# Attention results kept as channel rows through HBM, and a head's value product in two bursts

## What is computed

```python
def proj(W, b):
    return (x @ W.T + b).reshape(B, S, H, hd).transpose(0, 2, 1, 3)
Q, K, V = (proj(Wq, bq), proj(Wk, bk), proj(Wv, bv))
scores = jnp.einsum('bhqd,bhkd->bhqk', Q, K) * scale
attn = jax.nn.softmax(scores, axis=-1)
out = jnp.einsum('bhqk,bhkd->bhqd', attn, V)
out = out.transpose(0, 2, 1, 3).reshape(B, S, D)
return out @ Wo.T + bo
```

## Time and profile before

| | |
|---|---|
| time, three runs | 2012.56, 2013.42, 2052.93 us (median 2013.42) |
| profiled execution, its own time | 2010.89 us |
| its span, first to last instruction | 2008.9 us |
| granted TensorE clock over the span | 0.940 |
| busy: PE, DVE, ACT, POOL | 88%, 57%, 44%, 20% |
| head loop, first unit to last value product | 103.7 to 896.5 us |
| output projection, to the last statistics | 897 to 942 us |
| experts, wavelet, experts | 942 to 2008.9 us |

### The profile page before, as it was taken

How to read it: one execution, slowest core, us unless ns; L and a number is a source line. 1 busy time by engine, 2 the same in 40 slices (tenths; PEclk the granted TensorE clock), 3 DMA queues, 4 the chain that set the end, 5 groups by cost and what they waited for, 6 DMA issues and landing times. The chain is left out here.

```text
span 2008.9 us, 36274 instructions
## 1 busy us (share of the span) xinstructions
PE 1763.1 (88%) x11202; PEld 1122.9 (56%) x11203; DVE 1146.1 (57%) x2473; ACT 887.8 (44%) x1306; POOL 408.6 (20%) x573
## 2 busy tenths in 40 slices
PE   7999999999999999988479999999999579944772
PEld 4523444444444444437368888888888546943551
DVE  4688888888888888846821111111111287797223
ACT  3436666666666666664112333333332144230223
POOL 2310000000000000003013333333333100000782
PEclk9969999999999999999789999999999879977896
DMA  5501111111111111106624443344344300024544
GB/s 196 181 18 36 36 32 32 32 32 34 35 34 32 32 32 33 35 23 201 228 86 117 101 116 104 109 110 110 111 105 114 93 6 1 2 84 147 87 54 168
DMA packets 101160, 157.44 MB, mean 78 GB/s; under 512 B 19984, under 2 KB 76624, under 8 KB 95728
## 3 DMA queue, kind: packets, MB, share of 16 engines
q1 hardware_dynamic: 70720, 120.30, 18.4%
q0 software_dynamic: 21696, 23.85, 7.5%
q10 hardware_dynamic: 8688, 12.58, 1.7%
HBM read 122.23 MB, written 48.37 MB: 85 GB/s over the span
## 5 line engine op out<-in xcount | busy, mean ns | idle before, releaser
L552 DVE TENSOR_REDUCE unit_max<-ps_ring 128x1 f32<-128x512 f32 x1024 | 639.3, 683 | 70.1 <-PE ps_ring L427 64.1
L538 ACT ACTIVATE w<-ps_scores 128x1024 f32<-128x1024 f32 x512 | 503.6, 1022 | 263.3 <-PE ps_scores L504 260.4
L427 PE MATMUL ps_ring<-k_stack,q_stack 96*128 96x512 bf16 x1024 | 367.6, 393 | 17.6 <-POOL v_padded L390 7.6
L504 PE MATMUL ps_scores<-q_stack,k_stack 98*128 98x512 bf16 x1024 | 307.5, 382 | 2.6 <-ACT w L538 2.5
L1486 PE MATMUL m_ps_h<-m_xt,m_w 128*128 128x256 f32 x1248 | 278.6, 382 | 0.8 <-DVE m_xt L1537 0.8
L1498 PE MATMUL m_ps_y<-w,m_ht 128*128 x1248 | 275.8, 379 | 0.0
L449 PE MATMUL ps_o<-w,v_padded 128*32 128x256 f32 x4096 | 261.9, 385 | 0.0
L1486 PEld LDWEIGHTS m_ps_h<-m_xt,m_w 128*128 128x128 f32 x1248 | 239.0, 192 | 34.2 <-DVE m_xt L1537 1.2
L1498 PEld LDWEIGHTS m_ps_y<-w,m_ht 128*128 128x128 f32 x1248 | 234.2, 190 | 30.3
L427 PEld LDWEIGHTS ps_ring<-k_stack,q_stack 96*128 96x128 bf16 x1024 | 98.8, 97 | 259.0 <-DVE unit_max L552 177.2
L1518 ACT ACTIVATE m_ht<-m_ps_h,m_w 128x256 f32<-128x256 f32 x312 | 130.7, 470 | 144.8 <-PE m_ps_h L1486 144.8
(11 more groups left out here) (263 smaller groups left out, 1624.2 us busy)
## 6 DMA issues: line engine op xcount, KB each, us to landing
m_w<-in_w SPq DMA_DIRECT2D x39, 1028.0 KB
rows<-g_rows SPq DMA_DIRECT2D x16, 512.0 KB, 3.0
y<-sums SPq DMA_DIRECT2D x16, 512.0 KB, 7.1
q_parts<-qk_part SPq DMA_DIRECT2D x16, 384.0 KB
k_parts<-qk_part SPq DMA_DIRECT2D x16, 384.0 KB
q_stack<-q_parts SPq DMA_DIRECT2D x64, 96.0 KB
k_stack<-k_parts SPq DMA_DIRECT2D x64, 96.0 KB
xt<-in_xt ACTq DMA_DIRECT2D x8, 512.0 KB, 10.0
```

What stands on the lines that cost most here:

```text
L427: nc.tensor.matmul(out[:, :], qs[0:STACK, u, qt * P:(qt + 1) * P], ks[0:STACK, u, half * HALF:(half + 1) * HALF], start=True, stop=True).t ...
L504: mm = nc.tensor.matmul(p_s[kt % 2][:, half * HALF:(half + 1) * HALF], ks[:, u, kt * P:(kt + 1) * P], qs[:, u, half * HALF:(half + 1) * HALF],
L538: nc.scalar.activation(pt[:, kt, :], p_s[kt % 2][:, :], ACT.Exp, scale=SCALE)\
L552: nc.vector.tensor_reduce(unit_max[:, u % 2, half, qt:qt + 1], src[:, :], axis=AX.X, op=ALU.max).then_inc(ring_used, 1)
```

## The change

1. `EDGES` becomes (0, 4, 8): the value product of a head is two bursts of four tiles, one after step 5 and one after step 1 of the next head.
2. The fold is gone, on TensorE and on VectorE. SP stores each head's copied strips to HBM as they are (`store_o`; `o_raw` holds 32 rows of 1024 queries a head, of which rows 0 to 15 are the result's channels and row 16 the divisor).
3. Groups are of `HEADS` = 8 heads; one written out, six turns of the loop, one written out. In a group SP reads back the eight heads of the group before as 128 channel rows, and their divisors as 128x64 (`load_block`). VectorE takes the reciprocal of the divisors (after head 2 of the group), SP stores it and reads it back repeated for 16 rows (`store_reciprocals`, `load_reciprocals`), and VectorE multiplies 128x1024 into `c.o_t` (`scale_block`, after head 5). The eighth block is left for the output stage.
4. At a group's last unit two places of the ring's count are skipped, so that a turn of the loop is a multiple of three: product and reduction count 3 there (`taken`).
5. `stage_output` uses `c.o_t` directly as the stationary operand: no gathering, no transposes, no copies. Wo, the bias and the first x are loaded, and their bias added, during the last group. There are four buffers of x and four PSUM banks for products, and the loops are written out.

```diff
@@ constants @@
+HEADS = 8
+BLOCKS = 8
@@ new helpers @@
+def load_block(sp, c, g):
+    raw = c.o_raw[bass.ds(g * HEADS, HEADS), :, :]
+    sp.dma_start(c.raw[:, :, :].rearrange("p j f -> p (j f)"), raw[:, 0:HD, :]).then_inc(c.raw_loaded, 16)
+    sp.dma_start(c.den[:, :], raw[:, HD, :]).then_inc(c.den_loaded, 16)
...
+def scale_block(v, c, kb):
+    def split(x):
+        return x.rearrange("p j (b q) -> p j b q", b=2)
+    return v.tensor_tensor(c.o_t[:, bass.ds(kb, 1), :].rearrange("p a (b j q) -> p (a j) b q", b=2, j=4),
+                           split(c.raw[:, :, :]), split(c.inv[:, :, :]), ALU.mult).then_inc(c.scaled, 1)
@@ stage_attention @@
-        GROUPS = NH // SLOTS
-        FOLD_AT, ROWS_AT, COPY_AT = 4, 2, 1
-        EDGES = (0, 3, 6, KT)
+        GROUPS = NH // HEADS
+        ROWS_AT, COPY_AT = 2, 1
+        SPARES = -HEADS * (2 * KT + 1) % RING
+        EDGES = (0, KT // 2, KT)
...
+        def taken(last, u, kt, kind):
+            return 1 + SPARES if (u, kt, kind, last) == (HEADS - 1, KT - 1, "max1", False) else 1
@@ SP @@
+                def store_o(n, u):
+                    sp.wait_ge(o_copied, n + 1)
+                    sp.dma_start(c.o_raw[bass.ds(n + HEADS, 1), :, :].rearrange("a r (j f) -> (a j) r f", j=4), o_sb[:, u % 2, :])\
+                        .then_inc(c.o_stored[u % 2], 16)
...
+                        if not first:
+                            if u == 1:
+                                for p in range(2):
+                                    sp.wait_ge(c.o_stored[p], g * (HEADS // 2 * 16))
+                                sp.wait_ge(c.scaled, g)
+                                load_block(sp, c, g)
+                            if u == 3:
+                                sp.wait_ge(c.inverted, g)
+                                store_reciprocals(sp, c, g)
+                            if u == 4:
+                                sp.wait_ge(c.inv_stored, g * 16)
+                                load_reciprocals(sp, c, g)
+                        if not (first and u == 0):
+                            store_o(n - 1, u + 1)
@@ TensorE @@
                             if kt == 1 and not (first and u == 0):
                                 pv(n - 1, u + 1, BURSTS - 1)
-                            if kt in (4, 7):
-                                pv(n, u, (kt - 4) // 3)
-                            emit(kt, ("fold",))
+                            if kt == 5:
+                                pv(n, u, 0)
@@ VectorE @@
-                            elif kind == "fold":
-                                normalise(n - 2, g * 2 + (u // 2 - 1), at - 1, src)
...
+                        if not first and u == 2:
+                            dve.wait_ge(c.den_loaded, g * 16)
+                            nc.vector.reciprocal(c.rden[:, :], c.den[:, :]).then_inc(c.inverted, 1)
+                        if not first and u == 5:
+                            dve.wait_ge(c.raw_loaded, g * 16)
+                            dve.wait_ge(c.inv_loaded, g * 16)
+                            scale_block(nc.vector, c, g - 1)
@@ stage_output, TensorE @@
+                for i in range(NT // 2):
+                    b, s = i // PAIRS, i % PAIRS
+                    wait_from(pe, summed, i - 3)
+                    pe.wait_ge(c.scaled, min(2 * b + 2, BLOCKS) + 1)
...
@@ stage_output, VectorE @@
+                dve.wait_ge(c.den_loaded, LAST)
+                nc.vector.reciprocal(c.rden[:, :], c.den[:, :]).then_inc(c.inverted, 1)
+                for i in range(NT // 2):
...
+                    if i == 5:
+                        dve.wait_ge(c.raw_loaded, LAST)
+                        dve.wait_ge(c.inv_loaded, LAST)
+                        scale_block(nc.vector, c, BLOCKS - 1)
```

More of the change, by code:

```diff
@@ L423, in claim, with max_unit @@
                     wait_from(pe, ring_used, at - RING + 1)
-                def max_unit(u, qt, half, at, out):
+                def max_unit(u, qt, half, at, out, count=1):
                     claim(at)
@@ L474, in body @@
                 def body(g, first, last):
-                    for u in range(SLOTS):
-                        n = g * SLOTS + u
-                        ahead = not (last and u >= 2)
+                    for u in range(HEADS):
+                        n = g * HEADS + u
+                        ahead = not (last and u >= HEADS - 2)
                         before = count_before(g, first, last, u)
@@ L702, in product @@
                                                   wo[:, k, :], start=(k == 0), stop=(k == KC - 1))
                     mm.then_inc(made, 1)
-                def pairs(b, first, last):
-                    for s in range(PAIRS):
-                        if not (last and s == PAIRS - 1):
-                            turn(b * PAIRS + s + 1, s + 1)
-                        product(b * PAIRS + s, s)
-                pe.wait_ge(loaded_w, 16)
-                turn(0, 0)
-                peeled_ends(pe, B, pairs)
```

296 lines of the change are left out of this document (135 added, 161 removed).

## The result

The changed kernel is slower: 2054.48 us median of 4 runs (2052.5 to 2055.13) against 2014.16 for the kernel before, a ratio of 1.0219, interval 1.0197 to 1.0242. The interval excludes no change; it does not quite exclude a difference under 2%. One of the four runs of before, 2052.93, was disturbed, and all ratios and intervals here are taken from undisturbed runs alone, so they are not quotients of the medians shown. The forecast was 2020 with a range from 1992 to 2038. The profiled execution has a span of 2053.1 us, 44.2 more than before.

The account below looks back on a forecast made before the run. The head loop was taken as bound by TensorE and VectorE's coupling through three banks, not either engine's work. Terms -33 + 33 + 5 + 11 + 1.5 + 0.5 - 11 = +7 on 2010.9 gave 2018, median 2020, range 1992 to 2038.

Parts of the forecast that it names:

- The coupling of the two engines by three banks: Head loop: VectorE starves during bursts, the ring holds TensorE between them; two-burst distances 1.61 or 1.56 us, heads 12.1.
- the bursts do pay: Rival, head loop: VectorE does not starve in longer bursts; 1962 us in full (chance 0.05), 1990 at half (0.11).
- 2 to 3.7 us at five jumps: Rival, loop's jumps back: TensorE and VectorE wait for the doubled body's instructions; +10 to +18 us, chance 0.20.
- The combination's distance: Head loop, VectorE: no longer behind a burst, the combination of maxima stretches a distance from 0.60 to 0.79 us.
- The two bursts: Head loop: two bursts for three make a head 12.1 us, 0.54 above one without a fold; +33 us over 61 heads.
- a turn's end: A group's last unit: TensorE's lead is lost once a group; 0.7 us times 7, +5 us (0 to 8).
- both divisions: VectorE in the loop: a block's reciprocal and multiplication stand between reductions; 1.6 us a group, +11 us for seven blocks.
- Stores and loads on SP: SP's queue ahead of the extra rows: at most 2 us of delay against some 5 of slack, 0 us.
- late rows: Rival, SP's queue: extra rows come late behind a head's store; slower than 2%, 2080 with 1 us, chance 0.04.
- The output stage: After the last burst: both engines' paths end in 33 to 35 us against 45; -11 us, bounds 0 and -13.
- two landings of some 2 to 3 us: Output stage's start: VectorE waits for the last block's divisors to be stored and loaded back, then 0.55 us.
- output stage no faster: Rival, output stage: bound by the flow of x and w2, no gain; 2031 us, chance 0.10.

Follow-up runs that it names:

- e11: The changed kernel with the head loop written out on all five engines; 2023.28 us, ratio to before 1.0063.
- e1: The changed kernel with only TensorE's turns written out, the other engines keeping their loops; 2028.81 us, ratio to before 1.0088.
- e2: e1 with the value product in three bursts again; 1976.17 us, ratio to before 0.9830.
- e4: The kernel before with two bursts of four tiles in place of three, fold and short loop kept; 2063.28 us, ratio to before 1.0260.
- e5: The changed kernel with three bursts again, TensorE's loop of eight heads kept; 1993.87 us, ratio to before 0.9935.
- e3: The kernel before with TensorE's loop in turns of eight heads, three bursts and fold kept; 2036.69 us, ratio to before 1.0139.
- e9: The changed kernel with the four expert weight loads moved behind the last load of x; 2051.38 us, ratio to before 1.0206.
- e6: e2 with the output stage reordered: pairs added before the last reciprocal, block multiplied later, half the weights behind the reciprocals; 1976.60 us, ratio 0.9828.
- e10: e7 and e8 together, with the expert weights loaded behind x; 1969.07 us, ratio to before 0.9793.
- e8: e6 with TensorE in a loop of four heads, fourteen turns, the other engines in turns of eight; 1975.36 us, ratio to before 0.9824.
- e7: e6 with the block's multiplication in the head loop on GpSimd instead of VectorE; 1974.16 us, ratio to before 0.9814.

## Why the prediction was wrong, point by point

**The coupling of the two engines by three banks: right.** Distances of 1.61 and 1.56, a head of 12.13 where 12.1 was forecast, and in e11 12.92, 12.54 and 13.27 for the heads with a group's end, a reciprocal and a multiplication, where about 13.3, 12.5 and 13.2 were named. The written-out kernel (e11) has its last value product 18.4 us later than before, where the sum gave +18; that the two agree to half a microsecond is luck, since the loop's start scatters by more. The rival "the bursts do pay" is refuted twice (e1 against e2, e4 against before). The row that looked like a reason for longer bursts, TensorE busy 360 of 365 us, was the time of products that wait their turn. The Trainium skill, page TensorEngine Tiling (Array Packing), section Key Properties, says that changing the tiling mode drains TensorE. The traces agree that entering and leaving a burst costs some 0.24 us: with four tiles the products ahead of and behind a burst start 2.18 us apart, as forecast (424.65 and 426.83 in the changed kernel). But removing one burst in three did not give back 15 us, it went with a loss of 50 (e1 against e2).

**The jump: the step that failed.** The sum has no term for the loop's jumps: it took them as free since the earlier trace rows show no instruction transfer. That row was of a body of 911 instructions. The rival gave "2 to 3.7 us at five jumps". The place was right and the size was not: the five turns with a jump lose 25.7 us (changed against e1), up to 5.6 each. The landing was sized about right, 3.5 us on the mean, 17.6 in all. What the rival lacked is the other 8 us, which go with the clock: after these standstills TensorE ran at 1.2 GHz for up to 6.8 us, a burst included, and VectorE stood 2.6 us more. The sign that it named, pieces of 16 KB all through the loop, came. Its chance of 0.20 was too low. The text named the body's doubling and the 11 pieces at first entry, and then let an absence of transfers at half the length speak for the longer body. The Trainium skill, page Runtime: NRT & Kernel Launch, section Instruction fetch mechanics, gives 2048 instructions for TensorE. The runs do not agree with it as the limit of a loop's body: 1783 (changed, e5) and 1819 (e3) were fetched anew each turn and 911 were not. The same section says that a jump to a target that is not held stalls until it has been fetched. The trace agrees: 3.59 us. On the engines other than TensorE the run with their loops kept (e1) shows none that is over 0.3 us.

**The tenth of a microsecond a head in the loop: not foreseen.** 12.23 against 12.13, 0.7 us a turn (100.06 - 99.38), some 4 us in six turns. (The last value products differ by 4.5, which also holds a difference at the start and one fall of the clock.) The combination's distance was measured ahead of the loop, where the earlier trace rows stand, and used inside it.

**The two bursts: direction right, and the prices right only together.** Taken alone they cost 50 us (e1 against e2), not 33, and the rest of the head loop gained 27 (e2 against before), not 15. The two together, +22.9 for e1, are near the forecast of +18. The reason is that the terms are not independent. With three bursts the third stands at the head's end and covers the combination and more; a turn's end costs 0.12 us, the reciprocal nothing, the multiplication 0.55. With two they cost 0.73, 0.30 and 1.17, against the forecast's 0.7 and, for both divisions, 1.6. So the terms were sized for the kernel with two bursts, and hold there; as prices of the fold's or the bursts' removal alone they would have misled. VectorE in e2, the reciprocal and, three heads later, the multiplication:

```profile
535.36 0.17 DVE L603 TENSOR_TENSOR row_max<-unit_max 128x8 f32<-128x8 f32 x1
535.46 0.55 DVE L638 RECIPROCAL o_rden<-o_den 128x64 f32<-128x64 f32 x1
535.93 2.43 DVE L595 TENSOR_REDUCE unit_max<-ps_ring 128x1 f32<-128x512 f32 x4
...
558.49 0.17 DVE L603 TENSOR_TENSOR row_max<-unit_max 128x8 f32<-128x8 f32 x1
558.95 2.54 DVE L595 TENSOR_REDUCE unit_max<-ps_ring 128x1 f32<-128x512 f32 x4 [0.30 <-PE ps_ring L486]
...
570.05 0.17 DVE L603 TENSOR_TENSOR row_max<-unit_max 128x8 f32<-128x8 f32 x1
570.25 1.22 DVE L154 TENSOR_TENSOR biases<-o_raw_in,o_inv_in 128x1024 f32 x1
571.39 3.18 DVE L595 TENSOR_REDUCE unit_max<-ps_ring 128x1 f32<-128x512 f32 x5
```

A plain head has the reduction 0.46 after the combination there, waiting for TensorE; with the reciprocal in between it is 0.57.

**Stores and loads on SP: right.** TensorE waited 0.8 us in all for the extra rows from 300 to 860 us, in two places. The slower rival that was named (late rows) did not happen.

**The output stage: mis-sized.** -4.0 instead of -11, inside its bounds. The step that was mis-sized is the landings: "two landings of some 2 to 3 us" (the last store, then the load of the divisors) were 3.4 and 5.7, so VectorE began 10.3 us after the last burst where the sum has 6.5. The reciprocals' own landing had no term; it took 10.2 us and cost a wait of 5.3. The 3.7 us of the earlier trace rows is a median over loads of x that the two buffers kept apart; here more were under way at once (the DMA share is 0.70 from 948 to 989 us, 0.61 in the earlier trace rows). That this is the cause was shown for the reciprocals in part only (e9: 8.2 us without the weights ahead). TensorE's start was right (2.0 us after the last burst, 1.5 forecast), and the four banks filled ahead. Both prices of a pair were somewhat high, which gave some of it back: VectorE needs 1.38 us (971.93 to 973.32) where 1.60 was read from the earlier trace rows, and the last pairs come 1.73 apart at full clock where TensorE's 1.85 was. Three orders of the loads (e6, e9, e10) moved the stage between 38.4 and 42.5 us. None reached 34, and each wait taken away came back at the next load. The rival "output stage no faster" was nearer in its mechanism, the flow of loads, than in its size, no gain.

**The account in us, on the profiled executions.** The forecast was 2018, the measured 2054.94, 37 more: jumps 25.7, the tenth a head some 4, the start and one fall of the clock some 3, the output stage 7, the rest of the program -3.

## What to carry to other kernels

Where two engines are coupled by a few buffers, grouping one engine's other work into longer bursts costs at every burst what the buffers don't cover, and can cost more than the saved bursts give back; and a burst that stands where the other engine has extra work pays for that work. Before a loop's body is doubled, ask what it costs if the body no longer stays at hand, on the engine with the most instructions; transfers that are absent at the present length say nothing about twice that length. The engine alone can be given a shorter turn than the others (e8). Prices for parts of one chain should be taken in the arrangement that the change leaves, since slack that hides one term is the slack that another has used up.

## What the runs showed of the hardware

- A TensorE body of 1783 to 1819 instructions in a loop was fetched anew in every turn, in pieces of 16 KB, with a standstill of 2.4 to 3.6 us at each jump back; bodies of four heads (911 in the kernel before; e8) were not. The other engines' bodies of eight heads caused no wait over 0.3 us (e1).
- A standstill of TensorE in a busy stretch can be followed by 3.4 or 6.8 us at 1.2 GHz. The clock fell after all five in the changed kernel (3.37 to 3.64 us), after all five in e9 (3.14 to 3.58), after three of five in e5 (2.76, 2.46 and 2.96, not 3.06 and 2.91) and after one of six in e3 (3.13, not 2.37 to 2.68). It also fell, for 3.4 us, in three places after a wait of 1.12 to 1.25 us for VectorE (changed, e9, e11), while most waits of that length were followed by nothing.
- Loads of 512 KB that landed 3.7 us after their issue in the output stage of before took 6.1 us (the first x of the changed kernel) to 10.4 us where more were under way at once (changed, e6, e9, e10).
- A multiplication of 128x1024 from SBUF on GpSimd beside VectorE's reductions from PSUM delayed neither: 2.37 us where GpSimd's addition of that size takes 2.36, and reductions of 685 ns against 684 in e6 (e7). On VectorE the same multiplication took 1.88 and 1.89 us beside GpSimd's additions (e6, e10) and 1.23 in the changed kernel.
